# A recommender tower on one Trainium2 core: eight embedding fields of the first chunk by one-hot products instead of gathers

## The reference

```python
e = stack([tbl_f[ids[:, f]] for f in range(32)], axis=1)      # (512, 32, 64): one row of each table for each sample
p, q = e[:, i, :], e[:, j, :]                                  # all 496 pairs i < j
z = einsum('bpj,bpj->bp', einsum('bpi,pij->bpj', p, w), q)     # z[b, pair] = p^T w[pair] q, w: (496, 64, 64)
h = concatenate([z, dense_ctx], axis=1)                        # (512, 512)
h = maximum(h @ W_top1 + b_top1, 0)                            # 512 -> 512
h = maximum(h @ W_top2 + b_top2, 0)                            # 512 -> 256
y = h @ W_top3                                                 # (512, 1)
```

## Time and profile before

| | us |
|---|---|
| median of 3 runs | 218.34 (218.11 to 218.46) |
| profiled execution | 218.69 |
| its span | 216.9 |
| TensorE busy | 191.2 (88%) |
| VectorE busy | 172.7 (80%) |
| ScalarE busy | 153.7 (71%) |
| GpSimd busy | 153.7 (71%) |
| all DMA | 15.23 MB, mean 70 GB/s |

### The profile page before, as it was taken

How to read it: one execution, slowest core, us unless ns; L and a number is a source line. 1 busy time by engine, 2 the same in 40 slices (tenths; PEclk the granted TensorE clock), 3 DMA queues, 4 the chain that set the end, 5 groups by cost and what they waited for, 6 DMA issues and landing times.

```text
span 216.9 us, 6361 instructions
## 1 busy us (share of the span) xinstructions
PE 191.2 (88%) x2142; PEld 130.4 (60%) x2142; DVE 172.7 (80%) x157; ACT 153.7 (71%) x1178; POOL 153.7 (71%) x192
## 2 busy tenths in 40 slices
PE   0119869989998989999999999999999999999985
PEld 0017446534765654875876756675587745687874
DVE  0004686898999979999997999899999966999811
ACT  2000267599999989999989679997798883619401
POOL 4777777777777777777777777777788878885200
PEclk9999997999999999999999999999999999999999
DMA  5676657557111111111111111111100000000000
GB/s 186 255 228 232 233 193 237 201 168 282 27 30 29 27 30 26 27 33 26 24 34 29 24 30 28 29 30 27 26 21 14 9 2 0 3 2 3 5 0 0
DMA packets 6434, 15.23 MB, mean 70 GB/s; under 512 B 2689, under 2 KB 2945, under 8 KB 5250
## 3 DMA queue, kind: packets, MB, share of 16 engines
q1 hardware_dynamic: 2306, 10.62, 13.6%
q0 software_dynamic: 4096, 4.20, 9.3%
HBM read 14.82 MB, written 0.00 MB: 68 GB/s over the span
## 4 chain that ended last, share of the span: by engine, by line
PE 68%; POOL 8%; DVE 8%; issue 6%; ACT 4%; DMA 3%; DVEq 0%
PE pu L531 23%; PE pu L523 22%; PE pz L544 11%; POOL emb L313 8%; PE pt L551 5%; ACT turned L342 4%; DVE turned L425 3%; DVE prod L443 3%; PE pt L563 2%; DMA emb<-in_tbl,idx 2%; PE pu L551 1%; DVE prod L439 1%; DVE zB L451 1%; PE pu L491 1%; PE pt L573 1%
## 5 line engine op out<-in xcount | busy, mean ns | idle before, releaser
L313 POOL DMA_INDIRECT emb<-in_tbl,idx x128 | 121.2, 947 | 41.2 <-issue 29.8
L342 ACT ACTIVATE turned<-turned 128x64 f32<-128x64 f32 x560 | 134.0, 245 | 1.8 <-DVE turned L425 1.8
L342 ACT ACTIVATION_READ_ACCUMULATOR turned<-turned 128x1 f32 x560 | 107.3, 192 | 0.0
L425 DVE TENSOR_TENSOR turned<-pu,emb 128x1024 f32<-128x1024 f32 x64 | 76.0, 1217 | 9.8 <-PE pu L523 9.8
L443 DVE TENSOR_TENSOR prod<-pu,eT 128x1024 f32<-128x1024 f32 x48 | 57.1, 1217 | 22.7 <-PE pu L531 22.5
L531 PEld LDWEIGHTS pu<-eT,ws 64*128 64x128 f32 x1024 | 64.3, 193 | 16.6 <-issue 11.6
L531 PE MATMUL pu<-eT,ws 64*128 64x128 f32 x1024 | 68.7, 283 | 4.0 <-ACT eT L332 1.7
L523 PE MATMUL pu<-ws,eT 64*128 64x512 f32 x256 | 67.7, 630 | 2.4 <-DVE prod L443 0.8
L523 PEld LDWEIGHTS pu<-ws,eT 64*128 64x128 f32 x256 | 22.5, 192 | 21.5 <-issue 20.1
L332 ACT COPY eT<-pu 128x128 f32<-128x128 f32 (+1 forms) x28 | 11.1, 398 | 34.1 <-PE pu L491 34.0
L299 POOL TENSOR_TENSOR turned<-turned 128x512 f32<-128x512 f32 (+4 forms) x50 | 30.3, 607 | 6.6 <-DVE turned L425 3.3
(11 more groups left out here) (27 smaller groups left out, 29.7 us busy)
## 6 DMA issues: line engine op xcount, KB each, us to landing
ws<-in_w SPq DMA_DIRECT2D x8, 1024.0 KB, 4.8
emb<-in_tbl,idx POOLq DMA_INDIRECT x128, 2.4
w1s<-in_w SPq DMA_DIRECT2D x1, 1024.0 KB
zT<-in_dense SPq DMA_DIRECT2D x1, 512.0 KB, 3.3
w2s<-in_w SPq DMA_DIRECT2D x1, 512.0 KB
idx<-in_ids SPq DMA_DIRECT2D x1, 64.0 KB, 2.0
identity<-in_ident SPq DMA_DIRECT2D x1, 64.0 KB, 1.9
w3s<-in_w SPq DMA_DIRECT2D x1, 1.0 KB
```

The costliest lines, as they stand in the source:

```text
L313: nc.gpsimd.indirect_dma_start(out=emb[:, c % EC, x, :], out_offset=None, in_=tables[x], in_offset=bass.IndirectOffsetOnAxis(ap=idx[:, c, ...
L342: i = nc.scalar.activation(t, t, ACT.Copy, accum_out=zB[:, b // NT % 2, b % NT * 16 + v:b % NT * 16 + v + 1])
L425: nc.vector.tensor_tensor(turned[:, b % RB, :, :].rearrange("p (x f) i -> p x (f i)", x=2), u.rearrange("p x s i -> p x (s i)"), e, ALU.mu ...
```

## The change

In chunk 0 eight fields with tables of 1000 rows are no longer gathered. Their tables are loaded whole, 125 partitions with 8 consecutive rows of 64 each. The ids of the 128 samples are repeated over the 125 partitions, and VectorE compares them with the number of the row that each partition and column holds: for each of the 8 rows of a partition a column of 128 zeros and ones. Eight accumulated products per field, table rows times these columns, put the 64 elements of all 128 samples on the partitions at which `transpose_x` would have put them, two fields side by side in 64 columns each. The fields are renumbered (`FIELD_AT`), so that the eight stand at positions 8 to 15, pairs 4 to 7. Turned units need gathered rows, so another 16 of the units are turned.

The first eight groups are all ahead of step 0, in the order `FIRST`: pairs 4, 5 (by products), 0, 1 (gathered), 6, 7 (by products), 2, 3 (gathered). Columns of four fields fit at once; the fifth waits until the first pair is done. SP's queue now has the list of ids, the row numbers and the eight tables ahead of `w`, and `w`'s pieces wait for other pairs. Five matmuls of `select` by 256 columns run on TensorE before the first group. The tables lie in buffers 6 to 9 of `turned`, the columns in 5 to 8 of `prod` and the list in 4.

The written order of the rest is changed with it: `ORDER`, `ROWS` (ScalarE 38 of 64 row sums where it had 35, VectorE 17 where 19, GpSimd 9 where 10; of chunk 0 VectorE 3 where 5), `SUMS_AT`, `X_AT`, `MLP_AT`, `Z_LATE`. All 16 sums of chunk 0 now come by its step 31, where 10 did.

```diff
+HOT_FIELDS = (1, 3, 7, 14, 15, 19, 20, 26)
+HOT_ROWS = 1000
+HP, HJ = 125, 8
+assert HP * HJ == HOT_ROWS
+HOT = range(8, 16)
+_REST = [f for f in range(FIELDS) if f not in HOT_FIELDS]
+FIELD_AT = _REST[:8] + list(HOT_FIELDS) + _REST[8:]
+def is_hot(c, k):
+    return c == 0 and 2 * k in HOT
...
-TURNED = [2, 3, 5, 9, 10, 11, 12, 13, 18, 19, 20, 21, 22, 26, 28, 29]
+TURNED = [2, 3, 4, 5, 8, 10, 12, 14, 18, 20, 21, 23, 24, 26, 27, 29]
...
+W_BEHIND = (1, 3, 8, 9, 10, 11)
...
+FIRST = (4, 5, 0, 1, 6, 7, 2, 3)
+assert XN[0] == 1
+GROUPS = [(0, k, 1) for k in FIRST + tuple(range(8, KP))]
+GROUPS += [(c, k, XN[c]) for c in range(1, BCH) for k in range(0, KP, XN[c])]
...
-X_AT = [[-1, -1, -1, -1, 1, 2, 3, 4, 6, 7, 10, 12, 15, 16, 19, 24], [28, 33, 39, 48],
...
+X_AT = [[-1, -1, -1, -1, -1, -1, -1, -1, 0, 5, 7, 9, 11, 13, 17, 20], [27, 31, 38, 45],
...
-SUMS_AT = ((3, 10, 11, 18, 20, 22, 28), (1, 6, 7, 11, 21, 22, 24, 25), (1, 7, 15, 19, 26), (0, 1, 10, 27, 31))
+WARM = 5
+SUMS_AT = ((5, 7, 9, 10, 17, 20, 23, 27, 31), (0, 5, 6, 12, 22, 30), (3, 10, 13, 26), (1, 7, 10, 13, 27, 31))
...
+        def hot_table(i):
+            return turned[0:HP, 6 + i // 2, 8 * (i % 2):8 * (i % 2) + HJ, :]
+        def hot_columns(i):
+            return prod[0:HP, 5 + i % 4, :, :, :].rearrange("p x s b -> p (x s b)")
+        def hot_list():
+            return prod[0:HP, 4, :, :, :].rearrange("p x s b -> p (x s b)").bitcast(I32)
+        def hot_group(i):
+            return GROUP_OF[0, HOT[i] // 2]
...
+            sp.dma_start(hot_list(), hot_ids.broadcast_to([HP, len(HOT) * P])).then_inc(s_hot_ids, 16)
+            sp.dma_start(rows_at[0:HP, :], hot_rows).then_inc(s_hot_rows, 16)
+            for i, x in enumerate(HOT):
+                sp.dma_start(hot_table(i), tables[x].rearrange("(p j) e -> p j e", j=HJ)).then_inc(s_hot[i // 2], 16)
+                if i == 3:
+                    sp.dma_start(identity[:], ident).then_inc(s_ident, 16)
             for g in range(NU // WU):
                 if g >= W_AT_ONCE:
-                    sp.wait_ge(s_emb[2 * (g - W_AT_ONCE) + 1], 16 * 2)
+                    sp.wait_ge(s_emb[W_BEHIND[g - W_AT_ONCE]], 16 * 2)
...
+                    if is_hot(c, x // 2):
+                        continue
...
+                if is_hot(c, k):
+                    nc.scalar.copy(eT[:, c % EC, k, :], pu[:, FILL["x", g] % UR, 0, 0, :]).then_inc(xt_read, 1)
+                    return
...
+            dve.wait_ge(s_hot_ids, 16)
+            dve.wait_ge(s_hot_rows, 16)
+            for i in range(len(HOT)):
+                if i >= 4:
+                    dve.wait_ge(xt_ready, hot_group(i - 4) + 1)
+                at = rows_at[0:HP, :]
+                nc.vector.tensor_tensor(hot_columns(i).rearrange("p (j b) -> p j b", j=HJ),
+                                        bass.AP(hot_list().tensor, hot_list()[:, i * P:(i + 1) * P].offset,
+                                                [hot_list().ap[0], [0, HJ], [1, P]]),
+                                        bass.AP(at.tensor, at.offset, [at.ap[0], [1, HJ], [0, P]]),
+                                        ALU.is_equal).then_inc(ones_ready, 1)
...
+                if is_hot(c, k):
+                    i = 2 * k - HOT[0]
+                    pe.wait_ge(ones_ready, i + 2)
+                    pe.wait_ge(s_hot[i // 2], 16 * 2)
+                    for j in range(HJ):
+                        for h in range(2):
+                            mm = nc.tensor.matmul(pu[EMB * h:EMB * (h + 1), FILL["x", g] % UR, 0, 0, :], hot_table(i + h)[:, j, :],
+                                                  hot_columns(i + h)[:, j * P:(j + 1) * P], start=(j == 0), stop=(j == HJ - 1))
+                    mm.then_inc(xt_ready, 1)
+                    return
                 to = turned_over(("x", g), n)
+                if g == GROUP_OF[0, 0]:
+                    pe.wait_ge(s_ident, 16)
...
-            pe.wait_ge(s_ident, 16)
             pe.wait_ge(selected, 2)
+            four = bass.AP(select[:].tensor, select[:].offset, [select[:].ap[0], [0, 4], [1, 64]])
+            for _ in range(WARM):
+                nc.tensor.matmul(pt[0:64, 0:2, :], select[:], four, start=True, stop=True)
...
+        "hot_ids": np.asarray(inputs["ids"])[:P, list(HOT_FIELDS)].T.reshape(1, len(HOT) * P),
+        "hot_rows": np.arange(HOT_ROWS, dtype=np.int32).reshape(HP, HJ),
+        "ids": np.asarray(inputs["ids"])[:, FIELD_AT].reshape(BCH, P, FIELDS).transpose(1, 0, 2),
```

More of the change, by code:

```diff
@@ L50 @@
 assert NU == 32 and NT == 16 and all(UNITS[u][0] == "four" for u in TURNED)
+assert all(2 * (UNITS[u][2] + i) not in HOT for u in TURNED for i in range(4))
 assert ZCH * P == FIELDS * (FIELDS - 1) // 2 + DENSE
-TURN_AT = [[2, 3, 7, 9, 10, 11, 12, 16, 17, 18, 20, 21, 22, 29, 30, 31], [5, 6, 7, 10, 11, 12, 13, 15, 18, 20, 22, 23, 25, 26, 29, 31], [2, 3, 7, 8, 9, 10, 11, 14, 17, 18, 23, 26, 27, 29, 30, 31], [0, 5, 6, 10, 11, 12, 13, 14, 15, 16, 17, 18, 19, 20, 24, 26]]
+TURN_AT = [[0, 2, 4, 6, 8, 9, 10, 13, 14, 17, 19, 21, 24, 27, 30, 31], [4, 5, 6, 7, 11, 14, 16, 17, 18, 20, 21, 22, 25, 29, 30, 31], [2, 6, 7, 9, 12, 13, 15, 17, 18, 19, 21, 22, 23, 25, 26, 30], [1, 4, 5, 6, 9, 10, 11, 14, 18, 19, 20, 22, 23, 25, 26, 27]]
 ORDER = []
@@ L58 @@
 STEP = {(_t // NU, _u): _t for _t, _u in enumerate(ORDER)}
-ROWS = [[('act', 4), ('act', 7), ('dve', 7), ('dve', 9), ('act', 12), ('act', 15), ('dve', 17), ('dve', 26), ('act', 16), ('dve', 33), ('act', 20), ('act', 27), ('act', 29), ('act', 30), ('act', 35), ('act', 36)], [('act', 40), ('dve', 39), ('act', 43), ('dve', 45), ('dve', 52), ('act', 44), ('act', 50), ('act', 51), ('act', 56), ('dve', 56), ('act', 57), ('dve', 66), ('act', 61), ('dve', 69), ('act', 64), ('act', 64)], [('act', 72), ('act', 75), ('dve', 71), ('dve', 73), ('act', 75), ('act', 78), ('act', 80), ('act', 81), ('pool', 28), ('dve', 89), ('pool', 30), ('act', 94), ('act', 95), ('dve', 98), ('act', 100), ('dve', 100)], [('pool', None), ('act', 106), ('pool', None), ('act', 107), ('act', 111), ('pool', None), ('pool', None), ('dve', 112), ('pool', None), ('pool', None), ('dve', 119), ('pool', None), ('act', 121), ('dve', 123), ('act', 125), ('pool', None)]]
+ROWS = [[('act', 0), ('act', 5), ('act', 8), ('act', 11), ('act', 14), ('act', 18), ('dve', 17), ('act', 21), ('act', 26), ('act', 28), ('act', 28), ('dve', 27), ('act', 33), ('act', 34), ('dve', 31), ('act', 42)], [('act', 44), ('act', 46), ('act', 47), ('act', 53), ('dve', 50), ('act', 54), ('dve', 53), ('act', 55), ('act', 57), ('act', 63), ('dve', 55), ('dve', 59), ('act', 67), ('act', 70), ('dve', 68), ('act', 72)], [('act', 75), ('act', 79), ('dve', 71), ('pool', 7), ('dve', 80), ('act', 84), ('act', 85), ('dve', 85), ('act', 86), ('pool', 20), ('act', 92), ('act', 97), ('dve', 89), ('dve', 93), ('act', 99), ('dve', 96)], [('pool', None), ('pool', None), ('act', 103), ('act', 109), ('pool', None), ('dve', 110), ('act', 114), ('pool', None), ('act', 115), ('act', 118), ('pool', None), ('act', 119), ('pool', None), ('dve', 122), ('pool', None), ('dve', 123)]]
 Z_LAST = 31
@@ L114 @@
 W_AT_ONCE = 2
+W_BEHIND = (1, 3, 8, 9, 10, 11)
 XN = [1, 4, 4, 4]
-GROUPS = [(c, k, XN[c]) for c in range(BCH) for k in range(0, KP, XN[c])]
+FIRST = (4, 5, 0, 1, 6, 7, 2, 3)
+assert XN[0] == 1
+GROUPS = [(0, k, 1) for k in FIRST + tuple(range(8, KP))]
+GROUPS += [(c, k, XN[c]) for c in range(1, BCH) for k in range(0, KP, XN[c])]
 NG = len(GROUPS)
-X_AT = [[-1, -1, -1, -1, 1, 2, 3, 4, 6, 7, 10, 12, 15, 16, 19, 24], [28, 33, 39, 48], [60, 61, 71, 74], [91, 92, 98, 109]]
-MLP_AT = [(7, 15, 27, 37, 54), (8, 9, 34, 38, 45), (14, 15, 19, 23, 27)]
+X_AT = [[-1, -1, -1, -1, -1, -1, -1, -1, 0, 5, 7, 9, 11, 13, 17, 20], [27, 31, 38, 45], [54, 63, 67, 80], [83, 93, 103, 109]]
+MLP_AT = [(14, 19, 26, 39, 51), (13, 16, 22, 29, 36), (10, 13, 17, 21, 25)]
 X_STEPS = [at for of_chunk in X_AT for at in of_chunk]
@@ L160, with dlrm_tower @@
 SUMS[NS] = list(range(_a, BCH * NA))
-Z_LATE = [2, 1, 1, 116]
+Z_LATE = [3, 1, 4, 291]
 Z_OUT = [Z_LATE[c] + min(t for t in SUMS if (c + 1) * NA - 1 in SUMS[t]) for c in range(BCH - 1)]
-def dlrm_tower(nc, tables, ids, w, dense, w1, b1, w2, b2, w3, ident, out):
+def dlrm_tower(nc, tables, ids, hot_ids, hot_rows, w, dense, w1, b1, w2, b2, w3, ident, out):
     with ExitStack() as ctx:
@@ L175, in sem @@
             return ctx.enter_context(nc.semaphore(name))
+        rows_at = sb("rows_at", [P, HJ], I32)
         idx = sb("idx", [P, BCH, FIELDS], I32)
@@ L202, in dlrm_tower @@
         s_emb = [sem(f"emb_in{i}") for i in range(BCH * KP)]
+        s_hot_ids = sem("hot_ids_in")
+        s_hot_rows = sem("hot_rows_in")
+        s_hot = [sem(f"hot_tables_in{i}") for i in range(len(HOT) // 2)]
+        ones_ready = sem("ones_ready")
         s_w = [sem(f"w_in{i}") for i in range(NU // WU)]
@@ L265, in _ @@
             sp.dma_start(idx[:], ids).then_inc(s_idx, 16)
-            sp.dma_start(identity[:], ident).then_inc(s_ident, 16)
```

(12 more changed lines are left out.)

## The result

The changed kernel takes 225.7 us (225.18 to 226.23, 4 runs), the kernel before 218.38: a ratio of 1.034, 95% interval 1.031 to 1.037. It is slower, as forecast, but by 7.3 us where 2.2 were forecast. The profiled execution took 225.18 us with a span of 223.4.

The account below looks back on a forecast made before the run. Bounds: gathers before the first multiply, VectorE and TensorE in chunk 0, TensorE in chunks 1 to 3. Sum: 30.3+43+135.2+10.6 = 219.1, with 1.8 outside 220.9, less 0.35 to the median: 220.5 us; range 214.0 to 225.0.

Parts of the forecast that it names:

- Five engines: Transfers of 125 partitions on SP's queue use five of 16 DMA engines; the tables' 2.56 MB take 19.5 us.
- The last table is there at 25.7: Table loading: data from 2.7 us, plus 19.5 transfer, 2.5 for gathers, 1 for smaller packets.
- The forecast's own sign: Sign of five engines: DMA share near 0.3 between 8 and 25 us, with over 100 GB/s and no more.
- The fourth hot group at 2.8 us: TensorE's last pair of table products, after the last table: 2.8 us, between the two clocks, ending at 28.5.
- Transposes, hand-over: After the last hot group: transposes to 29.1, a unit of 1.1 us and a hand-over, first multiply at 30.3.
- Compares in VectorE's empty time: Eight VectorE compares, 9.7 us together, covered by VectorE's empty time before the first multiply.
- Chunk 0 at 43: From first multiply to 33rd: 43 us, bounds 40.5 and 45.7, with VectorE's work 39.7.
- chunks 1 to 3 at 135.2: The stretch after chunk 0: 138.2 less 3.0 of TensorE's sums and transposes moved out, 135.2 us.
- ScalarE's 11.5 us more: ScalarE takes 38 row sums, not 35, 11.5 us more work; counted as nothing, bounds 0 and 3.
- The eight gathers that went: Chunk 0 issues 24 gathers, not 32: 10 us less on GpSimd, worth something only while chunk 0 waits for gathers.
- The rival of sixteen engines: Tables go over all sixteen DMA engines: first multiply at 18.5, time 208.8 us; chance 0.13.
- The range, to 225.0: Range of the whole forecast time, 214.0 to 225.0 us, leaving out sixteen engines, weight loads and one engine.

Follow-up runs that it names:

- the two splits: Changed kernel with the list of ids and each table loaded in two transfers: 112 and 13 partitions, 213.67 us; 100 and 25 partitions, 216.73 us.
- With w behind the tables: Changed kernel, but SP waits for the last table before it issues the first piece of w: 221.91 us.
- With the gaps filled: Changed kernel plus 8 and 10 more selector matmuls on TensorE ahead of the third and fourth hot groups: 224.53 us.
- with memsets: Tables loaded as halves of 64 partitions, with eight memsets in place of the compares: 269.75 us, while the kernel before took 263.34.

## Why the prediction was right in its sign and wrong in its size

- **Five engines: right.** The counts of packets show it, and the two splits turn the effect down in steps.
- **"The last table is there at 25.7": the step that failed.** It came at 29.9. The sum let 2 KB packets cost 1 us over the rate of w's, and took the five engines to be theirs, since w's share there stands behind the tables. It put w's packets beside the tables at nothing, without a reason; by the order of the queue they can only have been on the other eleven engines. They slow the tables: 6.4 and 7.0 us for two where 4.4 had been the pace. With w behind the tables the last one was there at 25.9, 0.2 from the forecast. That is 4.2 of the 4.9 us. The forecast's own sign shows the gap: a DMA share near 0.3 from 8 to 25 us has no room for w, and the share was 1.03 to 1.04 from 20 to 30. That 25.9 fits to 0.2 is in part luck: at 4.4 us for two tables, 2.56 MB take 22.0 us where the sum had 23.0, and data then flowed from 3.9 and not from 2.7 (an estimate from these rows).
- **The fourth hot group at 2.8 us, "between the two clocks": mis-sized.** It took 3.6, all at half clock, 0.8 more. With the gaps filled it took 2.0. The sum had w's first piece 2.5 us behind the tables; it came 2.9 behind, at 32.8 (18.6 us after its issue at 14.16), and the first unit, at 34.05, did not wait for it.
- **Transposes, hand-over: right**, 1.6 us from the end of the group to the first multiply where 1.8 was said.
- **Compares in VectorE's empty time: right on their own price** (9.35 us in all, 9.7 forecast), but they were not free: they lengthen gathers. Behind five engines nothing waited for these. In the splits it is a term.
- **Chunk 0 at 43, chunks 1 to 3 at 135.2: right**, 42.2 and 135.8. ScalarE's 11.5 us more cost nothing to be seen. The eight gathers that went saved nothing behind so late a start: even 32 would have been there in time (an estimate: the last would leave at 41.7, 3 us later with the lengthened gathers, and is wanted 20 steps of 1.3 us after 35.2). TensorE's own work in chunk 0 adds up to 38.6, not 38.7; nothing rests on it.
- **The rival of sixteen engines, 208.8, was too low**: 213.7 and 214.8 when it was made so. It had tables come at 421 GB/s and the eighth gather at 16.5; between 5 and 8 us tables came at 250 and 294, and the gather at 20.9 and 21.2.
- **The range, to 225.0, was too short on the slow side by 0.7 us.** It had no term for two streams that slow each other, only sizes around the terms that it had.

## What to carry to other kernels

Before a transfer is added, look at the count of its rows: 125 rows went over five engines here, and what was queued behind them waited. Cutting it in two, 112 and 13 rows, was worth 12 us. Ask also which other stream will run beside it: w's packets cost the tables 4 us here, though they stood behind them in the queue. Then ask what the next arrival is: as soon as the tables were quick, gathers behind 1 MB pieces that nobody needed yet set the start, and holding back w's second piece as well as its third gave another 2.5 us (213.85 to 211.38).

## What the runs showed of the hardware

- Two streams slow each other well below what one of them reached alone. Tables on five engines, without w, moved 0.51 MB in 4.4 us, 23 GB/s an engine; with w on the others all sixteen stood at a share of 1.03 to 1.04 and moved 270 to 277 GB/s, where w alone had moved 421. On sixteen engines tables without w reached 250 (64 and 64 rows) and 294 (112 and 13) between 5 and 8 us. Why packets of tables hold the total near 270 stays open: where they are written was changed and didn't bring the rate of w, where they are read and how large they are was not changed.
- A compare with both operands in SBUF can hold up a gather that GpSimd is issuing, from 0.95 to as much as 1.97 us, though not each (with w's second piece held, one of 0.94 ran from 14.01, amid compares from 11.66 to 16.51); the multiplies, with one operand in PSUM, don't: between 35 and 77 us all gathers of the changed kernel took 0.94 or 0.95. The Trainium skill, "SBUF — State Buffer", section "Who interferes with whom", says that VectorE with two SBUF inputs contends with GpSimd's reads; the trace agrees, for the issue of an indirect DMA. The section infers that a tensor_tensor leaves the making of descriptors alone all the same; here it doesn't, and the measurement decides. By the same section an instruction with at most one SBUF input doesn't contend outside the 2-port modes; with memsets all gathers took 0.94.
- SP's issues of 0.3 to 0.4 us grew to 4.1 (the row of 8.58 in the chain) while tables went to five engines; in the split of 112 and 13 they stayed near 0.4. So SP's queue stood still, and with it the issue of w, which came at 14.16 instead of the 6.3 that was forecast. Nothing in the changed kernel waited for w.
